# Expert rows scattered to token order during the expert tiles, the last 20 block sums on VectorE, and plain loads in place of 16 gathers

## The reference

```python
xn = _layernorm(x)
x = x + _L0_attn_ref(xn, ...) + _L0_ffn_ref(xn, ...)   # RWKV; experts, top 1 of 4:
#   g, u = x@Wg[e], x@Wu[e];  y = (silu(g)*u) @ Wd[e];  out = y[chosen] * top_w
xn = _layernorm(x)
x = x + _L1_attn_ref(xn, block_values, cols, rows) + _L1_ffn_ref(xn, weight, rram)
#   _L1_attn: 128 blocks of 64x64x16 taps, block n convolves channel group cols[n]
#   and is added to channel group rows[n]; rows/cols may repeat
```

## Time and profile before

| | us |
|---|---|
| median of 3 runs (lowest, highest) | 372.48 (371.27, 372.94) |
| the profiled execution | 371.43 |
| span of its instructions | 369.4 |
| PE busy in it | 342.5 |
| DVE / POOL / ACT busy | 236.5 / 220.0 / 125.4 |

### The profile page before, as it was taken

The page is one execution under the profiler, slowest core; times in us unless marked ns, Lnnn a source line. Parts: engine busy times, 40 slices in busy tenths (PEclk is TensorE's granted clock), DMA queues, the critical chain, the costliest instruction groups (busy, mean ns, idle before and its releaser), DMA issues.

```text
span 369.4 us, 6281 instructions
## 1 busy us (share of the span) xinstructions
PE 342.5 (93%) x1452; PEld 243.6 (66%) x1453; DVE 236.5 (64%) x389; ACT 125.4 (34%) x248; POOL 220.0 (60%) x191
## 2 busy tenths in 40 slices
PE   6899966789999999999999999999999948799996
PEld 5797755446656666556665566655678837688886
DVE  3836552899997898978879888221251548981134
ACT  4783307353352533525253261322222111300033
POOL 4851778487887888888888888875802760000000
PEclk9999996999999999999999999999999998999999
DMA  7995224599898576765558987689491338100015
GB/s 228 356 356 187 100 99 143 179 342 304 256 332 290 173 198 189 193 196 167 198 165 249 344 298 201 201 271 370 132 225 51 113 100 197 33 0 2 1 59 170
DMA packets 46791, 70.83 MB, mean 192 GB/s; under 512 B 5424, under 2 KB 24496, under 8 KB 46768
## 3 DMA queue, kind: packets, MB, share of 16 engines
q1 hardware_dynamic: 39904, 61.50, 53.7%
q10 hardware_dynamic: 5328, 4.85, 4.1%
q0 software_dynamic: 1536, 4.20, 3.5%
HBM read 56.76 MB, written 9.57 MB: 180 GB/s over the span
## 4 chain that ended last, share of the span: by engine, by line
PE 76%; DVE 9%; another core or an unknown queue 4%; DMA 3%; ACT 3%; issue 2%; POOL 1%; SPq 0%; DVEq 0%; POOLq 0%
PE py L889 17%; PE pg L861 16%; PE pu L861 16%; PE pt L872 4%; PE pu L993 4%; PE pt L993 3%; PE pg L791 2%; PE pu L791 2%; PE pr L985 2%; DVE big L1292 2%; PE py L801 2%; DMA big<-x 2%; DVE stats L1297 2%; PE pt L791 1%
## 5 line engine op out<-in xcount | busy, mean ns | idle before, releaser
L555 POOL TENSOR_TENSOR acc<-acc,ring 128x512 f32 x128 | 171.7, 1342 | 40.6 <-POOL acc L555 26.5
L861 PE MATMUL pg<-big,xs_t 128*128 x144 | 67.9, 594 | 0.8 <-ACT xs_t L649 0.8
L861 PE MATMUL pu<-big,xs_t 128*128 x144 | 67.7, 592 | 0.0
L889 PE MATMUL py<-big,h_t 128*128 x288 | 65.3, 380 | 0.0
L889 PEld LDWEIGHTS py<-big,h_t 128*128 128x128 f32 x288 | 54.6, 190 | 15.2 <-issue 8.7
L1221 DVE SCALAR_TENSOR_TENSOR th<-th,pu 128x512 f32<-128x512 f32 x36 | 24.5, 682 | 40.5 <-ACT th L660 40.5
L861 PEld LDWEIGHTS pu<-big,xs_t 128*128 128x128 f32 x144 | 27.4, 190 | 34.4 <-issue 34.4
L660 ACT ACTIVATE th<-pg 128x512 f32<-128x512 f32 x36 | 21.5, 597 | 78.4 <-PE pu L861 78.4
L861 PEld LDWEIGHTS pg<-big,xs_t 128*128 128x128 f32 x144 | 24.5, 190 | 18.2 <-issue 18.2
L1198 DVE RECIPROCAL big<-big 128x512 f32<-128x512 f32 x8 | 26.8, 3355 | 0.3
L872 PEld LDWEIGHTS pt<-ident,h 128*128 128x128 f32 x144 | 17.9, 141 | 12.8 <-issue 11.0
(11 more groups left out here) (269 smaller groups left out, 552.5 us busy)
## 6 DMA issues: line engine op xcount, KB each, us to landing
ring<-blocks SPq DMA_DIRECT2D x128, 256.0 KB, 3.1
big<-x SPq DMA_DIRECT2D x8, 512.0 KB, 7.1
big<-w_g SPq DMA_DIRECT2D x12, 256.0 KB, 5.2
big<-w_u SPq DMA_DIRECT2D x12, 256.0 KB, 4.6
big<-w_d SPq DMA_DIRECT2D x12, 256.0 KB, 4.8
slots_x<-h SPq DMA_DIRECT2D x1, 2688.0 KB, 10.8
xs<-slots_x ACTq DMA_DIRECT2D x19, 128.0 KB, 3.6
slots_y<-y_sb ACTq DMA_DIRECT2D x18, 128.0 KB, 3.1
```

Source lines behind the costliest of these rows:

```text
L555: g.tensor_tensor(a, a, ring[:, place, :].rearrange("p (j o) -> p j o", j=TAPS), ALU.add)\
L861: mm = t.matmul(dst[:, :], xs_t[:, par, k, :], big[:, ds(e * per_e + (w_at + k * FF + 512 * f), 512)], start=(k == 0), stop=(k == KC - 1))
L889: mm = t.matmul(py[:, 0:C], h_t[:, k, :], big[:, ds(e * per_e + (down_at + k * C), C)], start=(k == 0), stop=(k == KF - 1))
```

## The change

1. **Scatter in place of gather.** `slots_x` gets two more columns that carry the token's number, so each tile of the sorted list brings the numbers of its rows (`ids`). The stored result tiles 0 to 15 are loaded back into SBUF in six groups (`staged`, in the place of the first r, k, v pieces), and POOL scatters them by `ids` to a DRAM tensor in token order, `rows_y`. Tiles 16 to 18 are scattered from `y_sb` itself. At the end four plain loads of 512 KB, issued by SP, read `rows_y`. Unused slots go to two spare tiles of rows.
2. **Last 20 block sums.** POOL adds blocks 0 to 107 (`LEAD`); DVE adds the other 20, in five windows of four between the `act_half` calls of tiles 14 to 16 (`late_adds`, semaphore `s_bd`).
3. **Head.** `turn_slots(0)` no longer waits for all 24 pieces; the first gate products wait for the pieces of their own banks. On ACT, `scaled(0, 0)` moves behind the last piece and the first slot tile. On DVE the softmax sums and `hs` move ahead of the wait for `s_gt`.

```diff
+CX = C + 2
+LEAD, STAGED = 108, 12
+WINDOW = 4
+STAGES = ((0, 4), (4, 8), (8, 12), (12, 14), (14, 15), (15, 16))
@@ sync
+            def stage(g):
+                k0, k1 = STAGES[g]
+                for k in range(max(k0, k1 - 2), k1):
+                    sp.wait_ge(s_ys[k % 2], 16 * (k // 2 + 2))
+                    if k >= STAGED:
+                        sp.wait_ge(s_yt[k % 2], 16 * ((k - STAGED) // 2 + 1))
+                sp.dma_start(staged[:, k0 % STAGED:k0 % STAGED + k1 - k0, :],
+                             slots_y[k0 * P:k1 * P, :].rearrange("(n p) c -> p n c", p=P)).then_inc(s_st[g], 16)
+            refills(E3_TURN + 3, LEAD // RING + 1)
+            for g in range(3):
+                stage(g)
+            before_refill = {LEAD + RING: 3, LEAD + 3 * RING: 4}
+            for n in range(LEAD + RING, NBLK):
+                if n in before_refill:
+                    stage(before_refill[n])
+                sp.wait_ge(s_bd, n - RING - LEAD + 1)
+                sp.dma_start(ring[:, n % RING, :], blocks[n]).then_inc(s_bk[n % RING], 16)
+                q = n - RING * X_TURN
+                if q == 0:
+                    sp.wait_ge(s_wk, UNIT * 2 * ROUNDS)
+                if 0 <= q < len(late):
+                    sp.dma_start(*late[q]).then_inc(s_l1, 16)
+            stage(5)
...
-                    sp.wait_ge(s_gy[3], 64)
+                    for n in range(2):
+                        sp.wait_ge(s_yt[n], 16 * ((MT + 1 - n) // 2))
+                    for m in range(4):
+                        sp.dma_start(yg[:, 4 * m:4 * m + 4, :],
+                                     rows_y[4 * m * P:4 * (m + 1) * P, :].rearrange("(i p) c -> p i c", p=P))\
+                            .then_inc(s_gy[m], 16)
@@ gpsimd
-            with g.Fori(1, NBLK // RING) as i:
+            with g.Fori(1, LEAD // RING) as i:
...
+            def store_rows(s):
+                g.wait_ge(s_id, 16 * (s + 1))
+                if s >= 2:
+                    g.wait_ge(s_yt[s % 2], 16 * (s // 2))
+                for n, (k0, _) in enumerate(STAGES):
+                    if s == k0:
+                        g.wait_ge(s_st[n], 16)
+                g.indirect_dma_start(out=rows_y, out_offset=to_rows(s), in_=staged[:, s % STAGED, :],
+                                     in_offset=None).then_inc(s_yt[s % 2], 16)
...
+            for s in range(NT):
+                store_rows(s)
+            for s in range(NT, MT):
+                store_drained_rows(s)
-            for i in range(NT):
-                g.indirect_dma_start(out=yg[:, i, :], out_offset=None, in_=slots_y,
-                                     in_offset=bass.IndirectOffsetOnAxis(ap=pos_i[:, i:i + 1], axis=0))\
-                    .then_inc(s_gy[i // 4], 16)
@@ tensor
-            t.wait_ge(s_re, RP * ROUNDS)
             turn_slots(0)
+            t.wait_ge(s_re, RP * ROUNDS - 3)
             tile(0, 0, first_tile=True)
@@ vector
+                first = LEAD
                 for s in range(TAIL, MAYBE):
-                    tile(s)
+                    act_half(s, 0)
+                    if s > TAIL:
+                        late_adds(first)
+                        first += WINDOW
+                    act_half(s, 1)
+                    late_adds(first)
+                    first += WINDOW
+            def late_adds(first):
+                for n in range(first, first + WINDOW):
+                    slot = v.value_load(slot_i[0:1, n:n + 1], min_val=0, max_val=TRASH)
+                    v.wait_ge(s_bk[n % RING], 16 * (n // RING + 1))
+                    if n == LEAD:
+                        v.wait_ge(s_ba, LEAD)
+                    else:
+                        v.wait_ge(s_bd, n - LEAD)
+                    a = acc_runs[:, ds(slot, TAPS, 2), :]
+                    v.tensor_tensor(a, a, ring[:, n % RING, :].rearrange("p (j o) -> p j o", j=TAPS), ALU.add)\
+                        .then_inc(s_bd, 1)
-                v.wait_ge(s_gy[m], 64)
+                v.wait_ge(s_gy[m], 16)
```

More of the change, by code:

```diff
@@ L469, in _ @@
+            stage(5)
+            sp.wait_ge(s_bd, NBLK - LEAD)
+            for n in range(2):
+                sp.wait_ge(s_yt[n], 8 * NT)
             for s in range(SUPERS):
```

111 lines of the change are left out of this document (62 added, 49 removed).

## The result

The changed kernel takes 375.5 us (median of 13 runs, 373.8 to 378.1) against 372.5 (13 runs beside it, 369.8 to 374.9): ratio 1.0087, interval 1.0056 to 1.0118. It is **slower**, also by the half per cent that the prediction asked for (above 374.3); 365.5 was predicted, with a range from 362 to 373.5. The profiled execution has a span of 372.6 us against 369.4, 3.2 more.

What follows compares the result with a forecast made beforehand. PE's work plus 27 us of waits was taken to bound the kernel, except from 280.3 to 315.9. Span 369.4 - 0.8 + 1 - 7.2 = 362.4, plus 2.0 around it and 1.05 to the median: 365.5 us, range 362 to 373.5.

Steps and rivals of the forecast that it cites:

- Head, -0.8: Before the first gate product: dropping the wait ahead of the first input's turn saves nearly 0.89 us, taken as -0.8.
- Block sums, 0.9 us each: VectorE's added sums at the loop's end: 0.75 us plus slot load and semaphore, 0.9 each, a window of four 3.6 us.
- The loop: Expert tiles with added block sums and 4 MB more DMA: cost between 0 and +3 us, taken as +1.
- Scatters every 1.26 us: GpSimd beside the expert tiles: 16 scatters at 1.26 us each from about 237.6, all done by 270.
- my rival of the long train: Loop: scatters wait for slow landings, 14 take 34 us, PE's increments held, PE stands to about 274; near 386 us; chance 0.13.
- Tail, first group 1.8 earlier: After the last down product: last scatter lands in 2.5 us, load in 3.3, so group 0 starts at 288.1, 1.8 earlier.
- The lost wait at group 2, -5.4: Tail, VectorE's third group of sums: removing the gathers removes the lost wait there, 5.4 us of the tail's -7.2.
- Ends of the unknown costs: Whole kernel: 362.5 us (loop 0, load 3.2, 1 more in the head) to 371 (loop +3, loads 7.1).
- both rivals of the train: Loop: the row of scatters holds PE's increments; 371.4 us, chance 0.15, or if the row is long near 386, chance 0.13.
- The loads are no faster: Tail: the final loads take 7.1 us to land, giving 369.3 us; counted in the forecast's upper part, no separate chance.
- the windows are too long: Loop's end: VectorE sums wait for POOL's descriptor making, 1.7 us each, windows 6.6; PE stands 3.9; 369.9 us; chance 0.12.

Runs made afterwards that it cites:

- the run with three edits: Changed kernel with GpSimd's pause after head scatter 8, VectorE's last tiles behind the branch, and slot pair 0's copies behind the loads: 372.4 us, ratio 0.9978.
- the cuts: Kernel before, GpSimd waiting for the first eight indirect DMAs to land: in the head 363.5 us (0.979), in head and tail 365.0 (0.9763), in the tail 364.6 (1.0057).
- the 80 memsets: Kernel before with 80 small, never executed VectorE memsets at the start of the branch body that is jumped over: 374.9 us, ratio 1.0082.

## Why the prediction was wrong

The prediction's span of 362.4 us came out as 372.6. The 10.2 us between them are 5.0 in the head (4.2 lost, 0.8 gained forecast), 1.1 in the loop, 4.1 at the tail's first group, 0.4 behind the convolution's start, and 0.4 back at group 2.

- **Head, -0.8: the step failed.** The first gate product did start 0.75 us earlier (68.42; it was 69.17). What failed is "I let the gain through": I looked at VectorE's recurrence and not at its branch. The added sums cost nothing where they run and 5 us where they are jumped over, 4.2 of it on PE's path. That the longer body makes the stall is shown twice, by taking the length away and by adding it elsewhere. Its price in time is not its length: 2.0 us in the kernel before, and nothing to be seen when it is taken out of the changed kernel (375.4; 375.5), whose loop then waits for blocks.
- **Block sums, 0.9 us each: right** (0.69 and 0.21). SP issued block 112 at 245.68 and not at 242. The reason that I gave held, the store of tile 13, but that tile was 4.2 us late with the head; the scatters of tiles 0 and 1, which I had left out, set the request only when the head is early (243.83 in the run with three edits). The later blocks were late by the seven loads between the refills, which I had named and priced at nothing new. The loop took +2.1 against +1, inside its bounds of 0 to +3, but that was luck of a late head: from an earlier head PE waits 2 to 6 us for the window of block 112 alone (2.16, 5.80 and 6.03). The failure is of the sum: I added the loop's cost to the head's, and the loop's end had become nearly a fixed time, set by GpSimd's 108 sums and what waits behind them.
- **Scatters every 1.26 us: wrong**, 2.4, since each waits for the last but one to land. That is the pace of my rival of the long train, and I had left it out of the main sum. It moved the last copies out of the sums into the tail.
- **Tail, first group 1.8 earlier: wrong, 2.3 later.** The scatter of tile 18 landed in 4.8 us, not 2.5, beside eight copies of 256 KB, and the load took 4.4, not 3.3. With the copies out of its way the scatter took 2.4.
- **The lost wait at group 2, -5.4: right** (-5.8 to the convolution), and the cause named for it, a row of indirect DMAs that holds signals, is borne out by the cuts, on chips that hold. Two details were wrong: it is not PE's signals alone, and they are not all held until the row ends; the wait at 49.16 in the earlier trace rows, which I took for idle time, is a third such wait. The same text says of the head "the change leaves that as it is": true, and the larger prize lay there.
- **Ends of the unknown costs.** The lower end is misadded: 365.5 less 1 (loop), 0.1 (load) and 1 (head) is 363.4, not 362.5. The measured time lies above the upper end, so nothing hangs on it.
- **Rivals.** No unnamed wait stood in the loop while the scatters ran there, so both rivals of the train fell, though one of them gave the number nearest to the measured one (371.4). That it is their wider spacing that spares the loop was not tested. "The loads are no faster" and "the windows are too long" were nearer in kind: each gave about 370, one by a landing, one by VectorE. The sums took 0.69 us throughout, so the wait for GpSimd's descriptor making that the second supposed played no part. The real slower case, a branch, was not among them.
- What a chip that does not hold would do was in no case of mine. There the one gain of the change does not exist, and it costs 3.25%.

## What to carry to other kernels

Instructions added inside a branch body can be paid for by whoever jumps over the body: look at the rows between a branch and its target, and place common code once, behind the branches. Before work is moved to an engine that the bound engine waits for, follow its inputs back through the queue; if they end at another engine's pace, the place becomes a fixed time and later gains upstream are lost there. When rows of indirect DMAs run back to back and a wait ends at nothing the profile knows, cut the row once and measure again, on more than one chip.

## What the runs showed of the hardware

- A taken branch on VectorE over a body of 217 rows stood 5 to 5.9 us (77.83 in the changed kernel, 76.78 with the 80 memsets); over 137 rows or fewer nothing of it shows, the wait is the tanh's (1.01 and 0.92 us).
- In the first comparison and on the first two chips signals are seen late during 16 indirect DMAs issued every 1.26 us: PE's by 3.9 us (VectorE, 49.16) and 10.9 us (ScalarE, 57.70), VectorE's own by 3.94 us (298.32). One cut after the eighth took ScalarE's wait from 12.2 to 1.6 us and 2.1% off the time. On two others the uncut row shows none of it, in three kernels, and the kernel before is 2.8% faster there (362 against 372). What in the chip does it, and why not in all, stays open.
- A scatter of 128 rows of 1 KB lands in 2.4 us with no copies beside it (290.20 to 292.6) and in 4.8 us beside 2 MB of copies (289.03 to 293.8).
